# Vision-tower kernel, its front: kernel parameters loaded first, pixel sorts moved between patch copies, one product for both parts of a bias row, routed bias rows copied after the convolution

## The reference, cut to what matters

```python
# tokenizer: patches of 16 x 16, 7 x 7 of them
x = patches @ W_patch + b_patch + pos_embed            # (64, 49, 768) @ (768, 128)
coords = x @ W_coord + b_coord;  spinor = x @ W_spinor + b_spinor
K0 = sum(spinor * spinor, -1)
x_enh = (coords @ W_embed + b_embed) * K0[..., None] + x
h = layernorm(x_enh) * ln_gamma + ln_beta;  h = h @ W_out + b_out
# S4: a kernel K of 49 taps for each of 128 channels, from P, B, C, Lambda, log_step
g = 2.0 / step * ((1 - Omega) / (1 + Omega));  rec = 1.0 / (g[:, :, None] - Lam[:, None, :])
k00, k01, k10, k11 = (einsum('hn,hln->hl', v, rec) for v in (C*B, C*P, P*B, P*P))
K = ifft(c_scale * (k00 - k01 * k10 / (1 + k11))).real
h = h + causal_convolution(layernorm(h), K) + D * layernorm(h)
# mixture of experts: 2 shared experts, 8 routed ones, top 2 for a token
h = h + shared(layernorm(h)) + routed(layernorm(h))    # each expert: gelu(y @ w1 + b1) @ w2 + b2
```

## Time and profile before

| | us |
|---|---|
| median of 3 runs | 459.9 (452.2 to 461.32) |
| the profiled execution | 455.62 |
| its span in the profile | 453.8 |
| tile 0: DVE reads the first `embed` results (L846) | 49.13 |
| the same of tiles 1, 2 and 3 | 74.28, 100.28, 125.39 |
| first and last convolution on PE (L1375) | 152.38 to 182.28 |
| last routed product on PE | 422.3 |

### The profile page before, as it was taken

One profiled execution on the slowest core, in us unless ns is written; L12 is line 12 of the kernel. 1 busy time (PEld: TensorE's weight loads), 2 busy tenths in 40 slices (PEclk: granted clock), 3 DMA queues, 4 the chain that ended last, 5 costly groups with the idle time before them and its releaser, 6 DMA issues.

```text
span 453.8 us, 7260 instructions
## 1 busy us (share of the span) xinstructions
PE 374.6 (83%) x2562; PEld 309.2 (68%) x2562; DVE 182.8 (40%) x566; ACT 210.6 (46%) x424; POOL 189.8 (42%) x239
## 2 busy tenths in 40 slices
PE   0596998998949878389799999999999999999400
PEld 0464866676637766389588689889889888988300
DVE  0473486747687104754872221211211211211166
ACT  2560556846253621366362355445555445544153
POOL 6014135363411300340002567677677677674300
PEclk9997699999995998856998999999999999999955
DMA  8962045920030530040220254354454345454085
GB/s 202 253 193 72 2 142 156 328 107 1 0 108 8 179 136 1 2 142 1 79 80 8 51 192 147 117 202 159 127 181 173 131 157 203 105 149 145 23 260 165
DMA packets 22680, 55.43 MB, mean 122 GB/s; under 512 B 4807, under 2 KB 10365, under 8 KB 22649
## 3 DMA queue, kind: packets, MB, share of 16 engines
q1 hardware_dynamic: 17625, 46.25, 30.9%
q0 software_dynamic: 4480, 8.46, 7.5%
q10 hardware_dynamic: 544, 0.33, 0.4%
HBM read 28.63 MB, written 7.46 MB: 80 GB/s over the span
## 4 chain that ended last, share of the span: by engine, by line
PE 54%; issue 15%; DVE 9%; DMA 8%; POOL 5%; POOLq 3%; ACT 2%; DVEq 1%; SPq 1%; ACTq 0%
PE bank L1457 12%; PE bank L1480 12%; PE bank L1467 9%; DMA Xc<-in_x 3%; DVE dT L822 2%; PE bank L1432 2%; PE bank L1219 2%; PE bank L1437 2%; PE bank L1438 2%; PE bank L1439 2%; DMA rk<-rd 2%; PE bank L1252 2%; PE bank L1504 2%; PE bank L1515 2%; PE bank L1307 1%
## 5 line engine op out<-in xcount | busy, mean ns | idle before, releaser
L607 POOL DMA_INDIRECT xg<-yd,take x64 | 62.3, 973 | 65.1 <-DVE give L1140 45.9
L758 ACT ACTIVATE gf<-bank,wb 128x256 f32<-128x256 f32 x128 | 56.3, 473 | 56.9 <-PE bank L1457 56.9
L614 POOL DMA_INDIRECT rd<-og,give x64 | 63.2, 987 | 38.1 <-DVE og L1152 22.9
L1480 PE MATMUL bank<-wb,gf 128*128 128x128 f32 x512 | 62.5, 275 | 1.1 <-DVE og L1152 1.1
L1480 PEld LDWEIGHTS bank<-wb,gf 128*128 128x128 f32 x512 | 60.4, 192 | 1.4 <-DVE og L1152 1.4
L1457 PE MATMUL bank<-x,wb 128*128 128x256 f32 x256 | 60.6, 380 | 0.5 <-DVE x L1146 0.5
L1457 PEld LDWEIGHTS bank<-x,wb 128*128 128x128 f32 x256 | 47.0, 190 | 8.8 <-DVE x L1146 0.8
L758 ACT ACTIVATE gf<-bank,vcol 128x392 f32<-128x392 f32 x64 | 35.1, 588 | 37.0 <-PE bank L1439 36.9
L1467 PE MATMUL bank<-gf,ws 128*128 128x392 f32 x128 | 44.8, 492 | 0.0
L1146 DVE COPY x<-bank 128x256 f32<-128x256 f32 x32 | 13.6, 424 | 71.7 <-PE bank L1515 71.7
L1252 PE MATMUL bank<-patchT,Wp 128*128 128x392 f32 x96 | 37.3, 514 | 0.0
(11 more groups left out here) (250 smaller groups left out, 643.7 us busy)
## 6 DMA issues: line engine op xcount, KB each, us to landing
wb<-tab SPq DMA_DIRECT2D x32, 578.0 KB, 3.3
Xc<-in_x SPq DMA_DIRECT2D x12, 784.0 KB, 6.8
rk<-rd SPq DMA_DIRECT2D x8, 392.0 KB
Tt<-kpad SPq DMA_DIRECT2D x8, 300.1 KB
raw<-in_L_ffn_rw SPq DMA_DIRECT2D x1, 2048.0 KB, 10.3
out<-osb SPq DMA_DIRECT2D x8, 196.0 KB
Tt<-kpad SPq DMA_DIRECT2D x2, 600.2 KB
Tt<-kpad SPq DMA_DIRECT2D x1, 1200.5 KB
```

What stands on the lines that cost most here:

```text
L607: G.indirect_dma_start(out=xg[i % AHEAD][:, t, :], out_offset=None, in_=yd[:, :], in_offset=bass.IndirectOffsetOnAxis(ap=take[:, at:at + 1 ...
L614: G.indirect_dma_start(out=rd[:, :], out_offset=bass.IndirectOffsetOnAxis(ap=give[:, at:at + 1], axis=0), in_=og[i % 2][:, t, :], in_offse ...
L758: nc.scalar.activation(gf[q % 2][:, o, 0:width(q)], bank[o][:, 0:width(q)], ACT.Gelu, bias=bias1(n, o)).then_inc(act_done, 1)
L1480: last = MM(bank[7][:, D * t:D * (t + 1)], gf[q % 2][:, o, 128 * t:128 * (t + 1)], wb[i % WB][:, FO + F + o * D:FO + F + (o + 1) * D], sta ...
```

## The change

Five things are edited.

1. `lsraw`, `craw`, `lim` and `tan2` are SP's first four loads, ahead of the pixels; `craw` and `lim` leave ACT's queue. `ld_par` counts eight loads, `tan2` among them. DVE waits for `ld_tok` (now ten) only ahead of the bias rows.
2. ACT does `s2`, then `sort_pixels(0, 0)`, then the square of tile 0, then tile 0. The sorts of channels 1 and 2 follow the copies of t = 1 and t = 3; those of the next tile follow the copies of t = 4 and t = 5 and the first `xtok` copy.
3. The two products of `wce_T` move ahead of the last `project`, and a third product puts the same row at partition 32.
4. `bhi` and `blo` become partitions 0 and 32 of one tile `bhl` of 33 partitions, with zeros between; `ones` has 33 partitions too, and `add_bias` is one product. `brow` is loaded at both partitions.
5. The wait for `ld_rbb` and the copy of `rbb` move behind the eight adds of the convolution.

```diff
-        bhi = place("bhi", [1, 2, D], "k", F32R)
-        blo = place("blo", [1, 2, D], "k", F32R)
+        bhl = place("bhl", [LOW + 1, 2, D], "k", F32R)
...
+            load(lsraw[:, :], log_step.rearrange("(a b) -> a b", b=2), ld_par)
+            load(craw[:, :, :], C_.rearrange("(a b) n t -> a (b n) t", b=2), ld_par)
+            load(lim[:, :], Lambda_im.rearrange("(a b) n -> a (b n)", b=2), ld_par)
+            load(tan2[:, :], c_tan[0:1, :].broadcast_to([128, L]), ld_par)
             for c in range(C):
                 load_x(0, c)
                 if c == 0:
-                    load(lsraw[:, :], log_step.rearrange("(a b) -> a b", b=2), ld_par)
                     load(Wp[:, :, :], W_patch.rearrange("(t p) d -> p t d", p=128), ld_wp)
-            load(tan2[:, :], c_tan[0:1, :].broadcast_to([128, L]), ld_tok)
...
-            load(brow[:, 0, :], rows(b_embed), ld_tok)
-            load(brow[:, 1, :], rows(b_out), ld_tok)
+            for at in (0, LOW):
+                load(brow[at:at + 1, 0, :], rows(b_embed), ld_tok)
+                load(brow[at:at + 1, 1, :], rows(b_out), ld_tok)
...
-                    if t == (1 if first else 2):
-                        act.wait_ge(b_ready, k + 1)
-                        nc.scalar.activation(dT[:, :, :], bT[:, :, :], ACT.Square).then_inc(sq_ready, 1)
+                    if t == 2 and not first:
+                        square(k)
...
-                    if t % 2 == 1 and more:
+                    if t in (1, 3) and first:
+                        sort_pixels(0, t // 2 + 1)
+                    if t % 2 == 1 and more and not first:
                         sort_pixels(k + 1, t // 2)
+                    if t >= KT - 2 and first:
+                        sort_pixels(1, t - KT + 2)
                 for half in range(2):
...
+                    if first and half == 0:
+                        sort_pixels(1, C - 1)
...
-            for c in range(C):
-                sort_pixels(0, c)
-
             act.wait_ge(ls_T, 1)
             nc.scalar.activation(s2[:, :], bank[4][:, 0:HP], ACT.Exp, scale=-1.0).then_inc(s2_ready, 1)
+            sort_pixels(0, 0)
+            square(0)
             tile(0, True, True)
...
             def expert_biases():
                 V.tensor_copy(tab[:, :, 0:FO], vcol[:, V_B1 + FO * NS:V_B1 + FO * NX].rearrange("p (e o) -> p e o", o=FO))
+
+            def result_biases():
                 dve.wait_ge(ld_rbb, 16)
                 V.tensor_copy(tab[:, :, FO + F + FO * D:RW], rbb[:, :, :]).then_inc(biases_in, 1)
...
-            V.memset(ones[:, :].bitcast(F32), 1.0)
-            V.tensor_tensor(brow[:, 0, :], brow[:, 0, :], bank[6][0:1, D:2 * D], ALU.add).then_inc(tok_const, 1)
+            V.memset(ones[:, :].bitcast(F32), 0.0)
+            V.memset(bhl[:, :, :].bitcast(F32), 0.0)
+            dve.wait_ge(ld_tok, 16 * 10)
             dve.drain()
-
-            V.tensor_copy(bhi[:, :, :], brow[:, :, :])
+            for at in (0, LOW):
+                row = slice(at, at + 1)
+                V.memset(ones[row, :].bitcast(F32), 1.0)
+                V.tensor_tensor(brow[row, 0, :], brow[row, 0, :], bank[6][row, D:2 * D], ALU.add)
             dve.drain()
-            V.tensor_tensor(blo[:, :, :], brow[:, :, :], bhi[:, :, :].bitcast(F32), ALU.subtract).then_inc(bias_ready, 1)
+            for at in (0, LOW):
+                last = V.tensor_copy(bhl[at:at + 1, :, :], brow[at:at + 1, :, :])
+            last.then_inc(tok_const, 1)
+            dve.drain()
+            low_row = slice(LOW, LOW + 1)
+            V.tensor_tensor(bhl[low_row, :, :], brow[low_row, :, :], bhl[low_row, :, :].bitcast(F32), ALU.subtract).then_inc(bias_ready, 1)
...
                                 ALU.add).then_inc(conv_read, 1)
             dve.drain()
+            result_biases()
...
-                for n, part in enumerate((bhi, blo)):
-                    MM(dst[0:PAIR, :], ones[:, :], part[:, i, :].unsqueeze(1).broadcast_to([1, GP, D]), start=n == 0, stop=False)
+                MM(dst[0:PAIR, :], ones[:, :], bhl[:, i, :].unsqueeze(1).broadcast_to([LOW + 1, GP, D]), start=True, stop=False)
...
+            def embed_tables():
+                pe.wait_ge(wcT_ready, 1)
+                MM(bank[6][:, 0:D], wcT[:, :], we[:, :], start=True, stop=True)
+                MM(bank[6][0:1, D:2 * D], bccol[:, :], we[:, :], start=True, stop=True)
+                MM(bank[6][LOW:LOW + 1, D:2 * D], bccol[:, :], we[:, :], start=True, stop=True, tile_position=(0, LOW)).then_inc(wce_T, 1)
...
+                    if t == KT - 1 and first:
+                        embed_tables()
                     if t == KT - 1 and not first:
                         project_out(k - 1, 0)
                 project(k, KT - 1, first)
```

More of the change, by code:

```diff
@@ L89 @@
 NV = V_B1 + NX * FO
+LOW = 32
 def tower(nc, x, W_patch, b_patch, pos_embed, W_coord, b_coord, W_spinor, b_spinor, W_embed, b_embed,
@@ L261, in tower @@
         wsp = place("wsp", [D, DS], "k")
-        brow = place("brow", [1, 2, D], "su")
+        brow = place("brow", [LOW + 1, 2, D], "su")
         bsp = place("bsp", [PAIR, DS], "k")
@@ L284, in tower @@
         none = place("none", [PAIR, 2 * GP], "k")
-        ones = place("ones", [1, PAIR], "k", F32R)
-        bhi = place("bhi", [1, 2, D], "k", F32R)
-        blo = place("blo", [1, 2, D], "k", F32R)
+        ones = place("ones", [LOW + 1, PAIR], "k", F32R)
+        bhl = place("bhl", [LOW + 1, 2, D], "k", F32R)
         ksb = place("ksb", [L, D], "k")
@@ L629, in _ @@
             act.dma_start(ident[:, :], c_ident).then_inc(ld_par, 16)
-            for dst, src in ((praw, P_), (braw, B_), (craw, C_)):
+            for dst, src in ((praw, P_), (braw, B_)):
                 act.dma_start(dst[:, :, :], src.rearrange("(a b) n t -> a (b n) t", b=2)).then_inc(ld_par, 16)
-            for dst, src in ((lre, Lambda_re), (lim, Lambda_im)):
-                act.dma_start(dst[:, :], src.rearrange("(a b) n -> a (b n)", b=2)).then_inc(ld_par, 16)
+            act.dma_start(lre[:, :], Lambda_re.rearrange("(a b) n -> a (b n)", b=2)).then_inc(ld_par, 16)
             def copy_patches(k, t):
@@ L651, in sort_pixels, with square @@
                                Xc[c][:, :].rearrange("r (i w j) -> r i w j", i=P, w=NH)).then_inc(x_sorted[c], 1)
+            def square(k):
+                act.wait_ge(b_ready, k + 1)
+                nc.scalar.activation(dT[:, :, :], bT[:, :, :], ACT.Square).then_inc(sq_ready, 1)
             def back(k, half):
@@ L806, in _ @@
             V = nc.vector
-            dve.wait_ge(ld_par, 16 * 7)
+            dve.wait_ge(ld_par, 16 * 8)
             V.tensor_copy(lsrep[:, :, :], lsraw[:, :].unsqueeze(2).broadcast_to([HP, 2, N])).then_inc(lsrep_ready, 1)
@@ L942, in _ @@
             dve.wait_ge(s2_ready, 1)
-            dve.wait_ge(ld_tok, 16 * 9)
             dve.drain()
@@ L1219, in to_columns @@
                 return TP(dst, src, ident[0:rows_, 0:rows_])
-            pe.wait_ge(ld_par, 16 * 7)
+            pe.wait_ge(ld_par, 16 * 8)
             for i, src in enumerate((praw[:, :, 0], praw[:, :, 1], braw[:, :, 0], braw[:, :, 1], craw[:, :, 0], craw[:, :, 1],
@@ L1334, in tile @@
                 if first:
-                    pe.wait_ge(wcT_ready, 1)
-                    MM(bank[6][:, 0:D], wcT[:, :], we[:, :], start=True, stop=True)
-                    MM(bank[6][0:1, D:2 * D], bccol[:, :], we[:, :], start=True, stop=True).then_inc(wce_T, 1)
                     pe.wait_ge(tok_const, 1)
```

## The result

| | before | after |
|---|---|---|
| median | 457.6 us (452.2 to 461.3, 4 runs) | 442.8 us (442.5 to 444.7, 4 runs) |
| profiled execution / its span | 455.6 / 453.8 us | 442.5 / 440.7 us |
| DVE's first instruction | 15.41 | 6.58 |
| `s2` | 18.60 | 7.93 |
| first `embed` product on PE | 39.27 | 31.75 |

The account below looks back on a forecast made before the run. Bound: late parameter loads, half clock in tile 0's `embed`, and the `rbb` wait. Terms 7.1 + 5.1 + 3.4 + 3.3 = 18.9 us off 455.6 give 436.7; predicted median 438 us, range 430 to 448.

Parts of the forecast that it names:

- the second, the clock: First `embed`, tile 0: full clock after only 1.3 us of PE idle time, 4.8 us instead of 9.86; 5.1 us won.
- the first rival: `embed` of tile 0 still at half clock, from longer PE idle time or clock never granted: 445 us, chance 0.20.
- The front: Start to first `embed`: parameters land at 5.5, `embed` starts at 32.2 instead of 39.27; 7.1 us won, bounds 2.4 and 10.
- PE's slow start: PE's first patches and projections: slow for some 9 us from its start at 11.1, last `project` ending near 30.9.
- The clock in the `embed` of tile 0: First `embed`: PE idle 1.3 us instead of 4.11, so full clock, 4.8 us instead of 9.86; 5.1 us won.
- half clock all the same: Tile 0 `embed` at half clock, for instance with parameters 2 us late and 3.3 us idle: 445 us, chance 0.20.
- the "slower" rival: Half clock lasts on into the shared and routed products, 1 us per microsecond of full-speed PE work: 465 us, chance 0.04.
- The bias products: `embed` and `project_out`: one product fewer each at 0.31 us, 33 rows cost nothing; 3.4 us won, bounds 0 and 4.6.
- The 0.9 us for the two `project_out` at half clock: Last two `project_out`: removed bias products count 0.47 us each at half clock, 0.9 us within the 3.4 us.
- The convolution: No PE wait for `rbb`: 4.0 us won less 0.7 for its copy, 3.3 us; bounds 2.0 and 4.0.
- The rival, a wait for `Tt` in front of the fifth convolution: Convolution waits for a `Tt` block instead, losing some 2 to 4 of the 4.0 us: 442 us, chance 0.05.
- The signs that the forecast named: Trace marks: DVE near 5.5, `embed` near 32 with under 2 us idle, clock 1.00 from 30 to 45, `spinors` near 37.

Follow-up runs that it names:

- e2_tables_early: The `wce_T` products for the token tables one projection earlier on PE, against the changed kernel: median 437.9 us, ratio 0.957.
- after_again: The changed kernel run once more without further edits, against the kernel before: median 443.5 us against 456.6, ratio 0.969.
- e5_both: Changed kernel with POOL's tile 1 Cauchy terms behind the bias rows and `wce_T` products one projection earlier: ratios 0.963, 0.976 and 0.954 on three chips.
- filled kernel: `e5_both` plus six unused identity products in PE's idle time before the last tile's `project_out`: median 474.7 us against 475.1 without them, same chip.
- warm-gate kernel: Changed kernel plus nine unused identity products in PE's idle time ahead of the second norm's transposes: ratio 0.977 (0.965 to 0.988).

## Why the prediction was right in sum and wrong in steps

The range held and the forecast was 4.8 us low. The step that failed is the second, the clock, and the case that came true is in part the first rival. One sum is off: 436.7 and the 4.3 us by which the median lay above the profiled execution make 441.0, not the 438 that was forecast. And the dip read as slice 12 is in slice 13.

**The front (7.1 forecast, 7.5 measured).** The sum held, and that is luck, since its parts moved against each other. The parameters landed at 6.58, not 5.5, and so `Vq` ended at 21.07 instead of 19.8 and POOL's front at 30.29 instead of 29.0. PE's slow start, on the other hand, was over by 17.6 us (a projection in 1.50, the row above), some 5 us after PE's first patches and not 9, and the last `project` ended at 28.49 instead of 30.9. What was late came together with what was early: the bias chain started at 27.03, not at 29.4, and so met POOL's `bT`, which it had been forecast to miss. From `wce` to PE's start it took 4.7 us (27.03 to 31.75), against 4.1 before and 3.0 forecast.

The stall is the one the forecast had named by the Trainium skill, SBUF — State Buffer, section Who interferes with whom, and had put aside because it had POOL done before the chain starts. The runs agree with that page: two casts in 0.58 us with POOL idle and 1.79 with POOL at work, the two-input subtraction in 0.41 and 1.68. The copy of `wce`, which reads PSUM, took its 0.29 us even beside POOL's `QT` (at 25.39 in `e2_tables_early`).

**The clock in the `embed` of tile 0 (5.1 forecast, 1.3 measured).** The step reads "PE's idle time ahead of it becomes 32.2 - 30.9 = 1.3 us". It became 3.26: 0.45 less because `embed` came earlier, and 2.4 more because the last `project` ended earlier. An engine that is made faster ahead of a wait only waits longer, and here the longer wait cost the clock as well. The rival "half clock all the same" had named this number, 1.3 + 2.0 = 3.3 us, but hung it on parameters 2 us late; they were 1.1 us late and PE did the rest. Its 445 us is nearer to the result than the forecast's 438. And of the 1.3 us that the piece did win, 1.13 lies in the bias products (1.07 and 1.10 us before, 0.37 and 0.67 after, the first of these at full clock). With POOL held back the clock stayed and the piece took 4.92 us against 4.8 forecast, so the price of the clock was right. The condition was not: the forecast let the clock fall some 3.5 us into the idle time, and in the kernel with two bias products it fell 2.0 us into it (idle from 29.73, 0.89 as the mean of the microsecond from 31).

**The later dips** are what no step had. Full clock in tile 0 is in part given back later, by these traces: up to 405 us, the half-clock time is 58.0 us in before, 58.0 in after and 58.0 in `after_again`, 54.6 with POOL held back, 51.2 in `e5_both` (10 of it in the routed stage). The equal sums are no rule, since the other traces have 54.6 to 94.3. Before and after don't differ in it: what after has less of in tile 0 (10.2 us against 13.7) stands elsewhere. Of after's tiles the first two are 1.3 and 0.8 us shorter than before, the third is 1.0 us longer, with this in it (PE, after). Before had 0.89 us for the same seven transposes and a normal projection takes 1.50, so 1.7 us are lost:

```profile
93.84 1.57 PE L1239 MATMUL bank<-ident,Xr 112*128 112x112 f32 x7 [0.96 <-ACT patchT L641]
95.20 2.50 PE L1272 MATMUL bank<-patchT,Wp 128*128 128x392 f32 x4
```

And in the shared blocks after has a dip at 220 to 224 that before has not. One set of twelve shared products takes 3.78 us in it (219.90 to 223.68) and 2.24 in before (234.74 to 236.98), which is 1.5 of the 1.6 us lost there.

That is the "slower" rival in small: a half clock in the shared stage, priced at 1 us for each microsecond of full-speed work, but two short dips and not one long stretch. Why a dip comes at one place in one execution and not in another was not settled.

**The bias products (3.4 forecast, 1.3 in the piece).** Zero for the 33 rows was right. The price of 0.31 us for a product was too high, since a lone one takes 0.40 and only 0.23 goes with the second. The count fits: of the eight products from `spinors` of tile 1 to those of tile 3 the forecast had six count, which is 1.4 us by 0.23, and 1.0 to 1.4 were measured. Its eight in all make 1.8 us, not 2.5. In after the dip at 93 us takes 1.7 of it back. The 0.9 us for the two `project_out` at half clock was wrong altogether: from `spinors` of tile 3 to the convolution after wins 0.2 us, because DVE's `kt` is what ends last there, as the filled kernel shows (PE at full clock, then idle for 1.62 us).

**The convolution (3.3 forecast, 4.8 measured).** From the start of the fifth convolution to the transposes behind it, which were held up, it is 6.72 us before and 2.96 after (154.43 to 157.39): 3.76. The rest of the transposes and convolutions is 0.50 us shorter, the piece ahead of the fifth 0.84 (in before it held the 0.57 us wait for `Tt`, which after has at the first convolution instead, 1.12 us, ahead of this piece). The copy of `rbb` cost 0.26 us, not the 0.7 charged for it, because the issue time it follows was there before. The forecast took 4.0 for what was 4.26. The rival, a wait for `Tt` in front of the fifth convolution, is absent in after but stands in eight of the eleven traces with the late copy, as 0.8 to 1.4 us. So the 4.8 us are the lucky end: from the first convolution to the statistics these eleven take 27.7 to 30.2 us, with 28.9 in the middle, which is 3.8 us under before and near the 3.3 forecast.

**The signs that the forecast named.** DVE first at 6.58 (5.5), `s2` 7.93 (7), `Vq` 21.07 (20), no idle time between the fifth and sixth convolution, the `rbb` copy without a wait: these came. The first `embed` near 32 came, with 3.26 us of idle time and not under 2; the clock was 0.50 from 33 to 42, not 1.00; `spinors` came at 40.31, not 37; the product behind `add_bias` started 0.40 us after it, not 0.31.

## What to carry to other kernels

An idle time forecast as the difference of two ends needs both ends with their errors: here the idle time began 2.4 us earlier than forecast and ended only 0.45 earlier, and so 1.3 us became 3.3. Where small operations of DVE stand beside long ones of POOL on the path to PE, the order of POOL's work is worth a look: one wait that puts POOL's next-tile work behind the bias rows, with the tables one step earlier, brought the changed kernel from a ratio of 0.972 to 0.954, 0.963 and 0.976 on three chips. Filling PE's idle time with spare products held the clock only for the work right behind it, and twice won next to nothing, because another engine's chain set the end.

## What the runs showed of the hardware

- The granted clock fell for short stretches in the middle of work (at 91 to 95 us or 93 to 98, at 220 to 224), at other places in each execution, and the sum of half-clock time up to 405 us was 58.0 us in three executions of two kernels whose times differ by 13 us, but 51.2 to 94.3 over all the traces.
- The clock can fall after PE is at work again: the idle time of after ends at 31.75, the clock reads 1.00 until 32 and 0.50 until 42, though PE is busy for all of that time. In before it fell within the idle time (0.85 in the microsecond from 38, PE's start at 39.27), and with nearly the same idle time, 2.34 and 2.41 us, it fell in one kernel and not in another.
- Transposes of 98 columns and gate products of 8 columns ran at half clock for 20 us in the warm-gate kernel, although 6 us of dense products stood ahead of them and the first eight transposes still had full clock.
- A lone 512-column product of 98 weights ahead of 128-column ones occupied 0.40 us; two of them 0.63, with 1 row or with 33.
- The same kernel before took 456 to 458 us on three chips and 488 to 491 on two others, where the page's clock line has further dips in the routed stage (`e5_both`):

```profile
PEclk9999999999599965899899999899899989979955
```
